# Token-per-row tokenizer and norms, and routing spread over the attention's batches

## The chip, the cores and the metric

The kernel runs on one core of a Trainium2 chip. Its time is the device time in microseconds (us) of the program, the median of three executions; the profile is of one further execution. The engines are TensorE (PE), VectorE (DVE), ScalarE (ACT), GpSimd (POOL) and SyncE (SP), each with its own instruction stream; they wait for each other on semaphores.

## The reference

An audio tower of two layers on x of 8 x 750 x 128, which the tokenizer turns into 8 batches (B) of 376 tokens of 256 numbers. What this change touches is the first layer up to the routing of the experts:

```python
y  = einsum('bpd,de->bpe', patches_16x16(x), tok_W) + tok_b
h  = (y - mean(y)) * rsqrt(var(y) + 1e-6) * gamma + beta          # tokenizer with its norm
n  = layernorm(h)                                                  # eps 1e-5
q, k, v = rope(n @ Wq), rope(n @ Wk), n @ Wv                       # 16 heads of 64
h  = h + softmax(causal(q k^T / 8)) v @ Wo + bo
xf = layernorm(h);  probs = softmax(xf @ router_w + router_b)      # 4 experts
top_p, top_i = top_k(probs, 2);  gates = top_p / sum(top_p)
h  = h + sum_e gates[e] * ((silu(xf @ w1[e]) * (xf @ w3[e])) @ w2[e])
```

Behind it comes a second layer, a complex linear recurrence over the tokens (`recurrence`) and a feed-forward block with quantised weights and activations (`quantised_ffn`); neither is changed, but for where the recurrence's tables are computed.

## The kernel before

Activations lie in SBUF with the 256 features over partitions in two halves and the tokens in columns; a batch is 376 columns. `audio_tower` calls the stages one after the other, each a block of the five engines' programs that ends in a barrier:

- `tokenize` (L187): matmuls (L220) of patches and weights, while VectorE makes the recurrence's tables of powers (`recurrence_tables`, L94).
- `layernorm` (L236) twice, for the tokenizer (ln_tok) and ahead of the attention (ln_attn). A token is a column, so sums over its features are matmuls against ones (L275, L285); the centring (L301) and the reciprocal of the deviation (L310), over 128x376, are VectorE's, the multiplication (L323) GpSimd's, squares, roots and the affine part ScalarE's (L336, L347, L341). With the second pass `split_weights` (L365) splits four weight matrices into a high and a low part on ScalarE (L372), VectorE (L379) and GpSimd (L387): all products of the kernel are made of such parts, as high x high + low x high + high x low.
- `attention` (L391): per batch eight steps `step(b, c)`, one for each pair of heads, and a `begin`. In a step TensorE projects Q or K of a later head (`project`, L496), computes scores (L508 mask, L518), turns the probabilities (`turn`, L533) and multiplies them by V (`mix`, L550); at a batch's end comes the output product (`output`, L572), 24 matmuls of 376 columns for each half of the features. ScalarE copies the projection (`raw`, L633), splits Q and K (`qk_high`, L639), makes the exponentials (`probs`, L646) and the high part of the turned probabilities (`pt_high`, L655). VectorE swaps pairs for the rotation (`swap_pairs`, L755/756), finds the maxima (L763), makes `pt_low` (L779) and adds the residual (L790). GpSimd rotates (L727, L729, L731) and makes `qk_low` (L716). Every engine's order is that of the code. A loop on the chip runs over the batches; the last is written out. SyncE first loads the tables, then clears the 12,288 rows of `x_slots` (L472, four transfers), then loads `resid` (L475) for each batch.
- `dispatch` (L872): all batches once more: each is turned to a token per row (L947, L1000), its norm is made with `bn_stats` (L1043, L1044) and a root on ScalarE (L1005), it is turned back (L956) for the router's product (L966), the two best experts and their gates are found, positions come from a prefix sum (L979), and GpSimd scatters the rows to `x_slots` (L1158, indirect transfers).
- `expert_tiles` (L1165), `recurrence` (L1488), `quantised_ffn` (L1810).

## Time and profile before

| | |
|---|---|
| three runs | 1922.29, 1924.59, 1925.28 us; median 1924.59 |
| the profiled execution | 1914.82 us, of which its span is 1913.0 |
| busy, share of the span | TensorE 83%, VectorE 64%, GpSimd 55%, ScalarE 53% |
| mean granted TensorE clock | 0.906 of 2.4 GHz |

The granted clock is what the chip let TensorE run at, as a share of its full speed; 0.5 of it is the lower of its two levels, 1.2 GHz. In a row of the lines' view stand the line, engine, operation, destination<-source and count, then the busy time, the mean duration in ns, and the idle time of the engine just before, with what ended it. The page's 40 slices, of 47.8 us each, show the stages:

```profile
## 2 busy tenths in 40 slices
PE   7749898989898989897728999999999926698329
...
DVE  6756565656565656564643666666655549658896
...
PEclk9869998999998999999558999999999957799659
DMA  5153000000000000000336555555555521103123
```

The first two or three digits are the front, then attention up to the 19th, then the routing at low clock, the experts, the recurrence and the feed-forward block.

### The profile page before, as it was taken

The numbers are of one execution on the slowest core, as the hardware profiler recorded it, in microseconds if no ns is written. First come the engines' busy times: TensorE is split into PE (matmuls) and PEld (weight loads), VectorE is DVE, ScalarE is ACT, GpSimd is POOL, SyncE is SP. The second block draws the span as 40 slices with busy tenths as digits, with TensorE's granted clock in tenths as the row PEclk, the third lists the DMA queues.
The fourth block names the chain that finished last, engine by engine and source line by source line (L and its number), as shares of the span: only waits on it lengthen the run. The fifth ranks groups of instructions, "written<-read, shape, count | busy, mean of one in ns | idle before, by whom it ended". The sixth has DMA issues, their size and how long they took to land. (4 is left out here: it accounts for less than half of the span.)

```text
span 1913.0 us, 32335 instructions
## 1 busy us (share of the span) xinstructions
PE 1589.7 (83%) x11205; PEld 1476.6 (77%) x11205; DVE 1221.8 (64%) x2397; ACT 1011.1 (53%) x2168; POOL 1055.0 (55%) x827
## 2 busy tenths in 40 slices
PE   7749898989898989897728999999999926698329
PEld 4338898989898989897628999999999915598219
DVE  6756565656565656564643666666655549658896
ACT  3536564656564656563615555555555524448562
POOL 0486767676767676762355776676777736300000
PEclk9869998999998999999558999999999957799659
DMA  5153000000000000000336555555555521103123
GB/s 192 65 176 118 1 8 0 8 0 8 0 8 0 8 0 8 0 9 4 107 109 214 142 138 147 139 138 143 143 145 144 149 75 33 33 1 118 66 75 114
DMA packets 74599, 142.85 MB, mean 75 GB/s; under 512 B 7400, under 2 KB 50728, under 8 KB 73992
## 3 DMA queue, kind: packets, MB, share of 16 engines
q1 hardware_dynamic: 63992, 127.80, 21.5%
q0 software_dynamic: 10512, 13.83, 4.2%
q8 instruction: 53, 0.87, 0.2%
q14 instruction: 42, 0.34, 0.1%
HBM read 108.15 MB, written 46.83 MB: 81 GB/s over the span
## 5 line engine op out<-in xcount | busy, mean ns | idle before, releaser
L1463 POOL TENSOR_TENSOR expert_w_low<-expert_raw,expert_w_high 128x768 fp32r<-128x768 f32 x152 | 289.5, 1958 | 157.6 <-ACT expert_w_high L1322 156.7
L646 ACT ACTIVATE probs<-psum,neg_max 120x376 f32<-120x376 f32 (+2 forms) x384 | 176.4, 479 | 140.1 <-DVE neg_max L763 140.1
L716 POOL TENSOR_TENSOR qk_low<-rotated,qk_high 128x376 fp32r<-128x376 f32 x128 | 138.3, 1081 | 180.2 <-ACT qk_high L639 175.9
L533 PE MATMUL psum<-diag,probs 128*128 128x128 f32 (+2 forms) x1536 | 203.5, 283 | 26.9 <-DVE pt_low L779 22.7
L533 PEld LDWEIGHTS psum<-diag,probs 128*128 128x128 f32 (+2 forms) x1536 | 185.5, 194 | 36.2 <-issue 25.5
L779 DVE TENSOR_TENSOR pt_low<-psum,pt_high 128x752 fp32r<-128x752 f32 x128 | 120.5, 941 | 142.5 <-ACT pt_high L655 141.5
L1439 DVE TENSOR_TENSOR expert_act_low<-expert_act,expert_act_high 128x384 fp32r<-128x384 f32 x152 | 148.6, 977 | 79.6 <-ACT expert_act_high L1360 79.6
L1360 ACT ACTIVATE expert_act_high<-expert_act 128x384 fp32r<-128x384 f32 x152 | 79.8, 525 | 171.4 <-DVE expert_act L1434 171.4
L1281 PE MATMUL psum<-slots_high,expert_w_high 128*128 128x384 f32 x608 | 157.9, 340 | 9.0 <-DVE expert_act L1434 7.8
L1281 PE MATMUL psum<-slots_low,expert_w_high 128*128 128x384 f32 x608 | 155.3, 336 | 0.0
L1281 PE MATMUL psum<-slots_high,expert_w_low 128*128 128x384 f32 x608 | 155.1, 336 | 0.0
L655 ACT ACTIVATE pt_high<-psum 128x752 fp32r<-128x752 f32 x128 | 102.6, 801 | 97.8 <-PE psum L533 95.9
L727 POOL TENSOR_TENSOR rotated<-raw,rope_cos 128x376 f32<-128x376 f32 x128 | 127.4, 995 | 39.4 <-ACT raw L633 25.5
L1322 ACT ACTIVATE expert_w_high<-expert_raw 128x768 fp32r<-128x768 f32 x152 | 126.6, 833 | 33.6 <-DMA expert_raw<-in_experts 33.6
L731 POOL TENSOR_TENSOR rotated<-rotated,swapped 128x376 f32<-128x376 f32 x128 | 138.6, 1083 | 10.0
L1292 PE MATMUL psum<-expert_w_high,expert_act_high 128*128 128x256 f32 x456 | 134.2, 294 | 5.3 <-ACT slot_out L1342 3.8
L1434 DVE TENSOR_TENSOR expert_act<-psum,silu 128x384 f32<-128x384 f32 x152 | 84.7, 557 | 77.3 <-ACT silu L1356 76.8
L729 POOL TENSOR_TENSOR swapped<-swapped,rope_sin 128x376 f32<-128x376 f32 x128 | 132.6, 1036 | 0.0
L1292 PE MATMUL psum<-expert_w_high,expert_act_low 128*128 128x256 f32 x456 | 128.5, 282 | 0.0
L1292 PE MATMUL psum<-expert_w_low,expert_act_high 128*128 128x256 f32 x456 | 128.4, 282 | 0.0
L763 DVE TENSOR_REDUCE neg_max<-psum 120x2 f32<-120x752 f32 (+2 forms) x192 | 119.4, 676 | 6.5 <-PE psum L518 6.5
L550 PE MATMUL psum<-pt_high,v_high 128*128 128x376 f32 (+2 forms) x384 | 113.8, 296 | 2.2 <-DVE pt_low L779 2.2
(303 smaller groups left out, 4549.4 us busy)
## 6 DMA issues: line engine op xcount, KB each, us to landing
expert_raw<-in_experts SPq DMA_DIRECT2D x152, 384.0 KB, 3.1
x_slots<-in_c_slots SPq DMA_DIRECT2D x4, 3168.0 KB, 27.9
slot_rows<-x_slots SPq DMA_DIRECT2D x19, 396.0 KB, 4.8
up_spill<-held SPq DMA_DIRECT2D x5, 1128.0 KB, 4.9
held<-up_spill SPq DMA_DIRECT2D x5, 1128.0 KB, 5.7
patch<-in_patches SPq DMA_DIRECT2D x4, 752.0 KB, 6.8
hid_spill<-hid SPq DMA_DIRECT2D x1, 3008.0 KB, 8.5
resid<-hid_spill SPq DMA_DIRECT2D x8, 376.0 KB, 3.5
```

The source lines that it names most:

```text
L533: last = pe.matmul(psum[0:nj, BANK_PT + bank, at:at + ni], probs[0:ni, h % 2, src:src + nj], diag[0:ni, h % 2, it, 0:ni], start=True, stop ...
L646: last = act.activation(probs[0:ni, h % 2, at:at + P * it + ni], score_bank(h % 2, it), ACT.Exp, bias=neg_max[0:ni, h % 2, it:it + 1], acc ...
L716: pool.tensor_tensor(qk[1][:, c % 2, k, :], rotated[:, k, :], qk[0][:, c % 2, k, :].bitcast(F32), ALU.subtract).then_inc(qk_ready, 1)
L727: pool.tensor_tensor(rotated[:, k, :], raw[:, k, :], cos[:], ALU.mult).then_inc(rope_made, 1)
L729: pool.tensor_tensor(swapped[:, k, :], swapped[:, k, :], sin[:], ALU.mult).then_inc(rope_made, 1)
L731: pool.tensor_tensor(rotated[:, k, :], rotated[:, k, :], swapped[:, k, :], ALU.add).then_inc(rot_made, 1)
L779: dve.tensor_tensor(pt[1][:, h % 2, :, :], psum[:, BANK_PT:BANK_PT + 2, 0:TOK], pt[0][:, h % 2, :, :].bitcast(F32), ALU.subtract).then_inc ...
L1281: last = pe.matmul(psum[:, 2 * k + g % 2, 0:TILE_SLOTS], w[hw][:, f, at:at + P], xt[hx][:, i % 2, c, :], start=(n == c == 0), stop=(n == 2 ...
L1292: last = pe.matmul(psum[:, BANK_DOWN + s, 0:DIM], act_hl[ha][:, g % 2, P * s:P * (s + 1)], w[hw][:, f, 4 * P:4 * P + DIM], start=(n == f = ...
L1322: act.activation(w[0][:, g % RING, :], raw[:, g % RAW, :], ACT.Copy).then_inc(w_high, 1)
L1439: dve.tensor_tensor(act_hl[1][:, g % 2, :], act_f[:, g % 2, :], act_hl[0][:, g % 2, :].bitcast(F32), ALU.subtract).then_inc(low_made, 1)
L1463: pool.tensor_tensor(w[1][:, g % RING, :], raw[:, g % RAW, :], w[0][:, g % RING, :].bitcast(F32), ALU.subtract).then_inc(w_low, 1)
```

## The change

`tokens_in` takes the place of `tokenize` and both passes of `layernorm`. A token is a row there, so mean and variance of both norms come from `bn_stats` on VectorE, the reciprocal is over 128x3, and ScalarE scales a row with its own factor and shift. The batches go through as a pipeline, `for i in range(BATCH + 3)`, in which the second norm of batch i-2 and the turning back of batch i-3 stand beside the first of batch i; the weights are split from i = 2 on. h and the norm's result are stored in DRAM and loaded by batch in the attention.

In `attention` all batches are written out (no loop on the chip). The output is made with tokens in rows, 3 tiles of 24 matmuls of 256 columns. `dispatch` is gone: the routing of batch b-1 stands in steps of batch b. Step 0 has its statistics, step 1 the root on ScalarE (which loads a table, and reloads the exponential's behind it), step 2 the scaling, 3 and 4 the turning, then the router's product, the odds' exponential, the choice, and in step 7 the positions; the scatter of batch b-2 stands in GpSimd's row in batch b, ahead of head 6. The last batch's routing follows at the stage's end. Seven small transfers with the router's parameters (`params`) are issued by SyncE between the clears of `x_slots` and the first `resid`; VectorE waits for all of them before its first batch. The recurrence's tables are begun in `tokens_in` and doubled in VectorE's row in the expert stage (chunks from 120 on).

The diff, cut (`route` calls the turning, the product and the prefix sum of TensorE by step; `seventh_read` only waits):

```diff
@@ tokens_in, SyncE (in place of tokenize and two layernorm passes) @@
+                for i in range(BATCH + 3):
+                    if here(i):
+                        sp.wait_ge(h_made, i + 1)
+                        many, few = token_rows(h0_rows, i)
+                        sp.dma_start(many, h[:, i % 3, 0:2, :]).then_inc(stored[i % 3], 16)
+                        sp.dma_start(few, h[0:TILE_ROWS[2], i % 3, 2, :]).then_inc(stored[i % 3], 16)
+                    if here(i - 3):
+                        sp.wait_ge(x_kept, i - 2)
+                        sp.dma_start(x_dram[:, :, tokens_of(i - 3)], xt[:, (i - 3) % 2, :, :]).then_inc(x_stored[(i - 3) % 2], 16)
...
@@ tokens_in, ScalarE @@
+                for i in range(BATCH + 3):
+                    if here(i):
+                        deviation(0, i)
+                    if here(i - 2):
+                        deviation(1, i - 2)
+                    if here(i):
+                        scale_tokens(i)
+                    if here(i - 2):
+                        scale_rows(i - 2)
+                    if here(i - 3):
+                        keep(i - 3)
+                    if 0 <= i - SPLIT_FROM < len(matrices):
+                        split_high(i - SPLIT_FROM)
...
@@ tokens_in, VectorE @@
+                for i in range(BATCH + 3):
+                    if here(i):
+                        biased(i)
+                        stat(0, i, y[:, i % 2, :, :])
+                    if here(i - 2):
+                        dve.wait_ge(h_made, i - 1)
+                        stat(1, i - 2, h[:, (i - 2) % 3, :, :])
+                    if here(i):
+                        inverse(0, i, h_scaled)
+                    if here(i - 2):
+                        inverse(1, i - 2, x_made)
+                    if 0 <= i - SPLIT_FROM - 1 < len(matrices):
...
@@ attention, SyncE @@
+                for b in range(2):
...
                     sp.dma_start(x_slots[e * CAPACITY:(e + 1) * CAPACITY, :], a["c_slots"]).then_inc(slots_cleared, 16)
-                with sp.Fori(0, BATCH) as b:
-                    sp.wait_ge(out_kept, 2 * b + CR_OUT)
...
+                sp.dma_start(bo[:], a["token_rows"][:, 3, :]).then_inc(params, 16)
...
+                sp.dma_start(before_f[:], a["c_before"]).then_inc(params, 16)
+                sp.dma_start(h_rows[TOKENS:TOKENS + TILE_SLOTS, :], a["c_slots"][0:TILE_SLOTS, 0:DIM]).then_inc(params, 16)
+                for b in range(BATCH + 1):
+                    if b:
+                        sp.wait_ge(out_kept, T * b)
+                    if b + 2 < BATCH:
+                        sp.wait_ge(attn_x_low, b + 1)
+                        sp.dma_start(xin[:, b % 2, :, :], x_dram[:, :, tokens_of(b + 2)]).then_inc(x_loaded[b % 2], 16)
+                    if b < BATCH:
+                        many, few = token_rows(h0_rows, b)
+                        sp.dma_start(resid[:, 0:2, :], many).then_inc(resid_in, 16)
+                        sp.dma_start(resid[0:TILE_ROWS[2], 2, :], few).then_inc(resid_in, 16)
+                    if b:
+                        many, few = token_rows(h_rows, b - 1)
+                        sp.dma_start(many, h[:, 0:2, :]).then_inc(h_stored, 16)
+                        sp.dma_start(few, h[0:TILE_ROWS[2], 2, :]).then_inc(h_stored, 16)
                 sp.wait_ge(slots_cleared, 16 * EXPERTS)
+                sp.wait_ge(params, 16 * 7)
+                sp.wait_ge(h_stored, 32 * BATCH)
 
...
@@ attention, TensorE, project(b, n) @@
-                        pe.wait_ge(out_kept, 2 * b + CR_OUT)
-                    w = (wq, wk)[k]
+                    if n == 2 * LEAD and b:
+                        pe.wait_ge(out_kept, T * (b - 1) + 2)
+                    if 2 * LEAD <= n and b:
+                        seventh_read(pe, b, (n - 1) // 2 - LEAD)
+                    wqk = (wq, wk)[k]
                     for i, (hw, hx) in enumerate(three):
...
+                def ahead_of(b):
+
+                    pe.wait_ge(chosen_made, b + 1)
+                    for k in range(T + 1):
+                        some = range(min(k + 1, T))
+                        for j in some:
+                            n = TILE_ROWS[j]
+                            m = TILE_ROWS[k] if k < T else P
+                            last = pe.matmul(prefix(b)[0:m, k, :], (before if j == k else ones_b)[0:n, 0:m],
...
@@ attention, TensorE, step(b, c, more) @@
                         values((0, 1))
+                    if b:
+                        if more or ahead < 2 * PAIRS:
+                            pe.wait_ge(raw_made, 16 * b + ahead + 1 + CR_RAW)
+                        else:
+                            pe.wait_ge(raw_made, 16 * (b + 1) + CR_RAW)
+                        route(b - 1, c)
                     turn(b, 2 * c + 1)
                     mix(b, 2 * c)
                     if more or ahead < 2 * PAIRS:
...
@@ attention, ScalarE @@
+                def deviation(b):
+                    act.wait_ge(summed, T * (b + 1))
+                    act.activation(std[:], moments[:, :, 1], ACT.Sqrt,
+                                   bias=consts[:, EPS_LN:EPS_LN + 1]).then_inc(std_made, 1)
+
+                def scale_rows(b):
+                    act.wait_ge(rstd_made, b + 1)
+                    if b:
+                        act.wait_ge(scattered, 32 * T * b)
+                    for k in range(T):
+                        n = TILE_ROWS[k]
+                        act.activation(rows[0:n, k, 0:DIM], h[0:n, k, :], ACT.Identity,
+                                       scale=rstd[0:n, k:k + 1], bias=shift[0:n, k:k + 1]).then_inc(x_made, 1)
+
...
+                    if b and c == 1:
+                        deviation(b - 1)
+                    if b and c == 2:
+                        scale_rows(b - 1)
+                    if b and c == ROUTE_LOGITS:
+                        odds_exp(b - 1)
...
@@ attention, GpSimd @@
+                def scatter(b):
+                    u = b % 2
+                    if b == 0:
+                        pool.wait_ge(slots_cleared, 16 * EXPERTS)
+                    pool.wait_ge(slots_made, b + 1)
+                    pool.wait_ge(gates_made, b + 1)
+                    pool.wait_ge(x_made, T * (b + 1))
+                    for k in range(T):
+                        n = TILE_ROWS[k]
+                        for j in range(2):
+                            pool.indirect_dma_start(
+                                x_slots, bass.IndirectOffsetOnAxis(ap=slots_u[0:n, u, j, k:k + 1], axis=0),
+                                rows[0:n, k, :], None).then_inc(scattered, 16)
+
...
+                for b in range(BATCH):
                     for n in range(2 * PAIRS):
+                        if n == 2 * LEAD and b >= 2:
+                            scatter(b - 2)
                         k = n % 2
...
@@ attention, VectorE, end of step(b, c, more) @@
+                    if b and c == 0:
+                        stat(b - 1)
+                    if b and c == ROUTE_LOGITS + 1:
+                        choose(b - 1)
+                    if c == ROUTE_LOGITS - 1:
+                        add_bo(b)
...
@@ attention, VectorE, before its first batch @@
+                x_split(0)
+                dve.memset(ones_b[:], 1.0).then_inc(routing, 1)
+                link(dve.memset(rows[:], 0.0))
+                dve.wait_ge(params, 16 * 7)
+                dve.tensor_copy(before[:], before_f[:]).then_inc(routing, 1)
                 dve.tensor_copy(base[:], const("region"))
...
-                        place_rows((i - 9) // T)
+                dve.wait_ge(tables_in, 64)
+                dve.tensor_copy(mask[:], mask_f[:]).then_inc(masks_made, 1)
+                dve.tensor_copy(ident_b[:], ident_f[:]).then_inc(masks_made, 1)
+                for n in range(2 * LEAD):
...
@@ expert_tiles, VectorE, after the work of chunk g @@
+                    at = g - FIRST_TABLE
+                    if at == 0:
+                        follow(dve.tensor_copy(turn[:, :, :, 0], first[:]))
+                    if 0 <= at < 2 * DOUBLINGS:
+                        double_turns(at // 2, at % 2)
+                    if 2 * DOUBLINGS <= at < 2 * DOUBLINGS + HALVES:
+                        feeds(at - 2 * DOUBLINGS)
...
```

What stands in VectorE's row where attention begins; before, `x_low` is the first batch's split, `mask` and `ident_b` are made of the loaded tables, and L756 is `swap_pairs`:

```order
L750 TENSOR_TENSOR x_low<-held,x_high 128x752 [waits x_high,cleared]
L827 CAST mask<-mask_f 128x256 [waits tables_in]
L828 CAST ident_b<-ident_f 128x256
L755 MEMSET holder 128x1 [waits raw_made]
L756 STREAM_SHUFFLE swapped<-raw 128x376
```

And now:

```order
L956 TENSOR_TENSOR x_low<-attn_x_in,x_high 128x752 [waits attn_x_high,cleared]
L1156 MEMSET ones_b 128x128
L1157 MEMSET x_rows 128x792
L1159 CAST before<-before_f 128x128 [waits route_params,route_step_made]
L1160 COPY slot_base<-moe_consts 128x4
L1162 CAST mask<-mask_f 128x256 [waits tables_in]
L1163 CAST ident_b<-ident_f 128x256
L961 MEMSET holder 128x1 [waits raw_made]
L962 STREAM_SHUFFLE swapped<-raw 128x376
```

Four instructions were put ahead of the masks, and the first of the casts waits for `params`; the swaps stand behind it.

ScalarE's row at the end of step 1 and the beginning of step 2 of a batch before, and now:

```order
L633 ACTIVATE raw<-psum 128x376 [waits rot_made,proj_made]
L637 REGISTER_ALU
L639 ACTIVATE qk_high<-rotated 128x376 [waits scores_made,rot_made]
L660 ACTIVATE o_high<-psum 128x376 [waits mixed]
L655 ACTIVATE pt_high<-psum 128x752 [waits mixed,turned]
L633 ACTIVATE raw<-psum 128x376 [waits rot_made,proj_made]
L646 ACTIVATE probs,row_sum<-psum,neg_max 120x376 [waits max_made,turned]
```

```order
L786 ACTIVATE raw<-psum 128x376 [waits rot_made,proj_made]
L792 ACTIVATE qk_high<-rotated 128x376 [waits scores_made,rot_made]
L813 ACTIVATE o_high<-psum 128x376 [waits mixed]
L817 ACT_TABLE_LOAD
L817 ACTIVATE row_std<-row_moments,consts 128x3 [waits route_summed]
L808 ACTIVATE pt_high<-psum 128x752 [waits mixed,turned]
L786 ACTIVATE raw<-psum 128x376 [waits rot_made,proj_made]
L799 ACT_TABLE_LOAD [waits max_made]
L799 ACTIVATE probs,row_sum<-psum,neg_max 120x376 [waits turned]
```

Two table loads and the root stand between `o_high` and the next `probs`.

GpSimd's row between the heads 5 and 6 of a batch, before and now (from the third batch on):

```order
L731 TENSOR_TENSOR rotated<-rotated,swapped 128x376 [waits rope_made]
L716 TENSOR_TENSOR qk_low<-rotated,qk_high 128x376 [waits qk_high]
L725 REGISTER_ALU
L727 TENSOR_TENSOR rotated<-raw,rope_cos 128x376 [waits qk_ready,raw_made]
L729 TENSOR_TENSOR swapped<-swapped,rope_sin 128x376 [waits swap_made]
```

```order
L934 TENSOR_TENSOR rotated<-rotated,swapped 128x376 [waits rope_made]
L903 TENSOR_TENSOR qk_low<-rotated,qk_high 128x376 [waits qk_high]
L916 DMA x_slots<-x_rows,slots_u 12288x264 [waits route_gates_made,route_x_made,route_slots_made,slots_cleared]
L916 DMA x_slots<-x_rows,slots_u 12288x264 x5
L930 TENSOR_TENSOR rotated<-raw,rope_cos 128x376 [waits qk_ready,raw_made]
L932 TENSOR_TENSOR swapped<-swapped,rope_sin 128x376 [waits swap_made]
```

Six scatters stand between one head's `qk_low` and the next head's rotation.

## Rows read from the trace of the kernel before

**Rows 1.** Windows by stage: length, busy us, granted clock, DMA share, GB/s.

```profile
0.00:117.00 117.00, 70.69 (x192) 39.39 (x192) 85.86 (x145) 49.52 (x72) 39.46 (x24) 0.85 0.27 105
117.00:147.00 30.00, 22.30 (x72) 17.78 (x72) 9.02 (x29) 8.70 (x16) 23.90 (x24) 0.63 1.00 320
147.00:904.50 757.50, 712.90 (x5977) 673.14 (x5976) 471.16 (x1073) 438.75 (x1257) 507.18 (x491) 0.98 0.03 10
904.50:1001.50 97.00, 46.90 (x264) 39.73 (x264) 53.74 (x277) 40.97 (x94) 46.99 (x48) 0.51 0.32 104
```

**Rows 2.** Timeline, SyncE's queue, attention begins: start, duration, queue, line.

```profile
118.77 2.65 SPq L472 DMA_DIRECT2D x_slots<-in_c_slots  x4
121.79 0.64 SPq L475 DMA_DIRECT2D resid<-hid_spill  x1
```

**Rows 3.** Tile `resid`: its transfers from issue to landing.

```profile
DMA to landing us min/median/max: 3.4/3.5/41.6
```

**Rows 4.** Timeline where attention begins, VectorE and TensorE.

```profile
124.63 0.57 DVE L756 STREAM_SHUFFLE swapped<-raw 128x376 f32<-128x376 f32 x1
...
147.01 0.51 PE L508 MATMUL psum<-mask,ident_b 64*128 64x128 bf16 x12
```

**Rows 5.** Lines, 0 to 117 us: busy us, mean ns | idle before.

```profile
L310 DVE RECIPROCAL ln_attn_rstd<-ln_attn_std 128x376 f32<-128x376 f32 x8 | 19.7, 2480 | 0.9 <-ACT ln_attn_std L347 0.9
...
L301 DVE TENSOR_TENSOR hid<-hid,psum 128x752 f32<-128x752 f32 (+1 forms) x8 | 7.2, 900 | 10.3 <-PE psum L275 10.3
...
L379 DVE TENSOR_TENSOR L_attn_Wv_low<-L_attn_Wv_staged,L_attn_Wv_high 128x1536 fp32r<-128x1536 f32 x1 | 2.8, 2810 | 0.0
```

**Rows 6.** Lines, 904.5 to 1001.5 us, the stage `dispatch`.

```profile
L1158 POOL DMA_INDIRECT x_slots<-x_rows,slots_u x48 | 47.0, 979 | 69.2 <-DVE slots_u L1097 56.4 <-issue 12.5 <-DVE x_rows L1084 0.3
...
L966 PE MATMUL psum<-router_w,router_x 128*128 128x4 f32 (+1 forms) x96 | 20.4, 318 | 0.5 <-ACT router_x L1013 0.5
L956 PE MATMUL psum<-ident,x_rows 128*128 128x128 f32 (+1 forms) x48 | 16.0, 437 | 17.5 <-DVE x_rows L1050 17.5
...
L1043 DVE BATCH_NORM_STATS2 row_stats<-h_tm 128x6 f32<-128x256 f32 (+1 forms) x24 | 10.1, 421 | 6.4 <-ACT h_tm L1000 6.4
...
L1005 ACT ACT_TABLE_LOAD x7 | 9.0, 1283 | 0.1
...
L979 PE MATMUL psum<-chosen,ones_b 128*128 128x4 bf16 (+2 forms) x48 | 4.6, 190 | 0.0
L1044 DVE BATCH_NORM_AGGREGATE row_moments<-row_stats 128x2 f32<-128x6 f32 (+1 forms) x24 | 4.4, 182 | 0.8
...
L979 PE MATMUL psum<-chosen,before 128*128 128x4 bf16 (+1 forms) x24 | 3.8, 197 | 3.0 <-DVE chosen L1079 2.9
```

**Rows 7.** Timeline of one attention step: GpSimd, VectorE, TensorE.

```profile
731.05 1.00 POOL L727 TENSOR_TENSOR rotated<-raw,rope_cos 128x376 f32<-128x376 f32 x1 [2.06 <-ACT raw L633]
...
736.86 1.53 PE L533 MATMUL psum<-diag,probs 128*128 128x128 f32 x12
...
737.22 1.16 POOL L716 TENSOR_TENSOR qk_low<-rotated,qk_high 128x376 fp32r<-128x376 f32 x1 [3.17 <-ACT qk_high L639]
...
739.26 0.94 DVE L779 TENSOR_TENSOR pt_low<-psum,pt_high 128x752 fp32r<-128x752 f32 x1 [0.39 <-ACT pt_high L655]
...
741.04 1.16 PE L533 MATMUL psum<-diag,probs 128*128 128x128 f32 x8
```

**Rows 8.** Timelines of TensorE and ScalarE, up to the batch's end.

```profile
745.84 1.53 PE L533 MATMUL psum<-diag,probs 128*128 128x128 f32 x12
...
790.00 0.52 ACT L639 ACTIVATE qk_high<-rotated 128x376 fp32r<-128x376 f32 x1 [3.88 <-POOL rotated L731]
...
792.70 0.57 PE L533 MATMUL psum<-diag,probs 128*128 128x128 f32 x3 [2.89 <-DVE pt_low L779]
```

**Rows 9.** Tile `slots_u`: indirect scatters from issue to landing.

```profile
DMA to landing us min/median/max: 2.4/2.6/3.8
```

**Rows 10.** Line 1471: duration ns min/median/max of GpSimd's indirect transfers.

```profile
L1471 POOL DMA_INDIRECT h_rows<-slot_out,slot_ids x57: 1550/1690/1710, 1051.5 to 1542.0; - x57
```

1129 lines of the change are left out of this document (528 added, 601 removed).

## Prediction

> **What bounds the kernel now.** I read four views, coarse to fine. First the windows by stage [rows 1]. From 0 to 117 us (tokenizer, two norms, splitting the weights) VectorE is the busiest engine, 85.86 of 117 us. From 147 to 904.5 us, the body of the attention, TensorE is busy 712.90 of 757.50 us at a granted clock of 0.98, that is at the 2.4 GHz level: this stage is TensorE's, and GpSimd (507) and VectorE (471) stand behind it. From 904.5 to 1001.5 us, the routing stage, no engine is busy for even 60% of the time and TensorE's clock is 0.51, the 1.2 GHz level: this is a stage of handoffs. So the first and the fourth stretch can be cut, and what is put into the third is paid for unless it fits between TensorE's instructions.
>
> Second, the lines of the first stretch [rows 5]: the reciprocal over 128x376 costs 2.48 us and runs 16 times, 39.5 us of VectorE, to give one number per token. Third, the timeline of an attention step [rows 7, 8]. `turn` of even heads starts at 736.86 and at 745.84: 8.98 us a step. In it GpSimd waits 2.06 us before L727 and 3.17 us before L716, both for ScalarE, so GpSimd has no long reserve of its own; between two heads it is only a fraction of a microsecond ahead of the chain that feeds ScalarE's `qk_split`. `pt_low` ends at 739.26 + 0.94 = 740.20, the `turn` that follows starts at 741.04: 0.84 us of slack. Where the batch ends that slack is gone: TensorE stands 2.89 us for `pt_low` at 792.70, behind ScalarE, which stood 3.88 us for GpSimd's `rotated` at 790.00. Fourth, the start of the attention [rows 2 to 4], where the DMA engines are busy throughout (share 1.00 in [rows 1]).
>
> **The change part by part.** The sum is made against the profiled execution, 1914.8 us; the median of the runs is 1924.6, 0.5% above it.
>
> *Front.* With a token per row a norm's statistics are 3 `bn_stats` and 3 aggregates per batch, and the reciprocal is over 128x3. VectorE has per batch one addition over 752 columns (0.90, L301 in [rows 5]), two sets of statistics of 3 x 0.42 + 3 x 0.18 = 1.8, a little overlapped 1.7 [rows 6], and two small reciprocals with their shift, about 0.4 each: 5.1, and I take 5.3 for contention. Batches 0 and 1 have no second norm beside them, 3.6 each; six are at 5.3, 31.8; the first sums come at about 10.5; four weight splits in VectorE's row cost 1.7 to 3.3, around 2.3 each (2.81 for one in [rows 5]), 9.2; behind the last batch its second norm goes through VectorE, ScalarE, TensorE, a store and the stage's barrier, about 16. That is 10.5 + 7.2 + 31.8 + 9.2 + 16 = 74.7 in place of 117: -42.5. Bounds: -50 if the splits hide, -30 if ScalarE's and TensorE's chain per batch does not keep up.
>
> *A wait before the first batch.* Seven small transfers (`params`) are issued by SyncE behind the four clears of `x_slots`, and VectorE now waits for all seven before it casts the mask and makes the first `swap_pairs`; behind that wait stand all its rotations, hence GpSimd, ScalarE and the first scores. The row beside it: `resid`, issued at 121.79 behind the same clears, landed 41.6 us later [rows 2, 3], at 163.4, while every other one of the eight took 3.4 or so. `resid` wasn't needed then; `params` are. Counted from the stage's beginning at 117.0 [rows 1], the first `swap_pairs` ran 7.6 us in, at 124.63 [rows 4], and `resid` came 46.4 us in; I take 51 to 52 for the last of `params`, since seven transfers are issued and one of them writes 384 rows in DRAM. That is 51.6 - 7.6 = +44. The first scores, at 147.01 [rows 4], move by the same. Bounds: 0, if the small ones land in their 3.4 us, and +50. I take +44, because the one transfer behind those clears that the trace shows did wait for them.
>
> *TensorE's added work in the body.* Per batch: 12 logit matmuls of 0.318 twice over 8 batches is 20.4 / 8 = 2.55, the turning 16.0 / 8 = 2.0, the prefix (4.6 + 3.8) / 8 = 1.05 [rows 6], all at clock 0.51; 5.6 at half clock is 2.8 at 0.98. The output now comes as 24 x 3 matmuls of 256 columns, 18,432, for 18,048: 0.15 us. With the switch of operands between them I take 3.1, seven times: +22. TensorE is the bound there, so all of it counts. Bounds: +14 if the small ones overlap, +39 at half clock.
>
> *Waits added in the body.* Three inserts per batch, in three engines' rows, seven batches each:
> - ScalarE: a table load before the root (1.283 [rows 6]), the root, and a load again before the next exponential, together about 3.0 us ahead of `pt_high` and `probs`. The step has 0.84 us of slack at `pt_low` [rows 7] and some idle time of ScalarE before it: I take 2.0 of 3.0, 14 in all.
> - GpSimd: six indirect scatters of 0.979 [rows 6], with their issue (47.0 + 12.5) / 48 = 1.24 each, 7.5 us in one piece, ahead of `rotated` of head 6. Its idle time within the step is 2.06 + 3.17 = 5.2 [rows 7], so 2.3 us are late, six times (the last two batches' scatters stand elsewhere): 14. Beside VectorE's work an indirect transfer of the same form takes 1.69 instead of 0.98 [rows 10]; then the piece is nearer 12 and the delay 6.6.
> - ScalarE's `scale_rows` (3 activations, about 1.1) 0.6 x 7 = 4; VectorE's small chunks (statistics 1.7, choice 1.25, place 1.1) in its idle time, 0.4 x 7 = 3; register instructions of the old loop gone, -1.
> Sum +34. Bounds: 0, if TensorE's own added work of 3.1 us is where the others catch up, and +83 (below).
>
> *The tail in place of the routing stage.* 97.0 us [rows 1] go. In their place one batch goes through alone: statistics 1.7, root 0.3, inverse 0.4, scaling 1.1, turning 2.0, its copy 0.5, logits 2.7, weighing 0.65, table and exponential 1.5, choice 1.25, prefix 0.65, place 1.1, six scatters 7.5, landing 2.6 [rows 9], the gap that lies today between the last landing and the next stage 5.0, handoffs 1.5: 30.5. (Prefix, weighing, choice and placing are three to seven instructions of 0.16 to 0.21 us each, as the small ones in the view of [rows 6].) That is 97.0 - 30.5 = 66.5, call it -67. Bounds: -72 and -58 (scatters at 1.69 [rows 10] and half-clock handoffs).
>
> *Recurrence tables* move from the front, where they lay beside the tokenizer's DMAs, into VectorE's idle time in the expert stage: +1, between 0 and +5.
>
> Sum: -42.5 + 44 + 22 + 34 - 67 + 1 = -8.5, 1906.3 for a profiled execution, and with the 0.5% of the median above it **1916**.
>
> **The rivals.**
> *The wait at the start doesn't happen.* All the small transfers land in about 3.5 us like the seven later `resid` [rows 3] and only the queue's 7 issues are added. For: they are a few hundred descriptors against the clears' 12,288 rows. Against: the first `resid` is small too, and waited 41.6. The 44 us fall away: 1872.
>
> *The body absorbs its inserts.* TensorE's 3.1 us stand in the same steps as the inserts on ScalarE and GpSimd, and GpSimd's lateness is made up in its idle 5.2 us of each step after it. Against it speaks the stand of 2.89 us at 792.70, which GpSimd causes today without any insert. The 34 us fall away: 1882.
>
> *Slower: the inserts are paid in full.* GpSimd is needed once per head, and ScalarE, which feeds it, waits for it in turn; if the two are so locked that neither regains what it lost, each insert is a delay for TensorE: 5.4 on ScalarE (3.0, 1.1 for `scale_rows`, 1.3 for the load at the odds' exponential) and 3.1 on TensorE, seven times, and 7.5 on GpSimd, six times: 59.5 + 45 = +105 in place of +56. That is 49 more: 1965. The place is head 6 of each batch from the third on, where the scatters stand ahead of `rotated`. It decides from the point at which GpSimd's delay exceeds the chain's slack of 0.84 us and the idle time of the same step isn't usable, since it lies after ScalarE's own wait.
>
> *A longer table switch.* The trace has 14 table loads in the routing stage, 1.283 us each, with idle 0.1 before them [rows 6], and I count them so. If each switch cost 1.38 us more, 14 switches on ScalarE's path in the body would add 19: 1935. The Trainium skill, page "ScalarE: Activation LUTs", section "What ACT_TABLE_LOAD costs", says just that: about 1283 ns for the load and about 1380 ns for a drain. This trace agrees with the first number and shows no row for the second.
>
> **How the numbers follow.** Forecast 0.45, inserts in full 0.25, body absorbs 0.15, no wait at the start 0.10, longer switch 0.05. The forecast's own range, from its uncertain terms (front -30 to -50, waits in the body by some 15 either way), is 1898 to 1936. The range to 8 in 10 takes in the absorbing body below and, above, most of the way to the slower rival: 1882 to 1955. What a measurement can tell from no change is 0.2%, 3.9 us. Faster by more is below 1920.7: 0.25 of the forecast's 0.45, and the two cases below with 0.25, 0.50. Within 0.2% (1920.7 to 1928.5): 0.12 of the forecast's. Slower: its last 0.08, the inserts and the switch, 0.38.
>
> **What would show each step.** The attention's first DMA at about 75 us instead of 117. VectorE's first `swap_pairs` 45 to 55 us behind it, released by the transfers and not by ScalarE; if it follows in under 12 us, the second term is wrong. The windows of the body: its batch period 95 now, about 103 forecast (22 + 34 over seven), 98 if absorbed, 110 if in full; TensorE's idle time there put down to `pt_low` and `qk_low`, in the step of the scatters. From the last residual to the first transfer of the expert stage 30 us. The forecast is wrong if the body's period lies outside 99 to 107 or the start's wait outside 38 to 50.

## The result and the profile after

The changed kernel took 1938.71 us (median of four runs, 1933.20 to 1942.99) against 1924.09 for the kernel before; the ratio is 1.0072, interval 1.0047 to 1.0097. I forecast 1916 with a range of 1882 to 1955: the time lies inside the range, but the sign was wrong. Run again on another chip, the ratio was 1.0046 (1.0029 to 1.0062). The kernel before took 1925.3 us on the chip of e1 to e4 and 1913.1 and 1913.6 on those of the later timed runs, so runs are compared by their ratios and, within a trace, by stages.

The windows by stage of the changed kernel (stretch, length, busy us of the engines, granted clock, DMA share, GB/s), cut at the attention's beginning, its first `swap_pairs`, its last residual, the expert stage's first transfer and the recurrence's first load:

```profile
0.00:76.00 76.00, 36.88 (x144) 29.44 (x144) 50.12 (x178) 44.47 (x80) 35.55 (x27) 0.77 0.53 189
76.00:125.30 49.30, 6.71 (x18) 5.26 (x18) 3.21 (x11) 1.80 (x3) 3.68 (x3) 0.50 0.95 320
125.30:973.00 847.70, 770.29 (x6411) 717.41 (x6411) 568.88 (x1323) 478.37 (x1334) 562.94 (x553) 0.95 0.05 17
973.00:1000.50 27.50, 4.78 (x27) 4.25 (x27) 7.76 (x44) 4.34 (x8) 5.90 (x6) 0.57 0.13 44
1000.50:1569.80 569.30, 518.72 (x3342) 500.77 (x3342) 361.53 (x602) 283.71 (x526) 374.27 (x209) 0.97 0.52 137
```

They answer to [rows 1]. The expert stage, which [rows 1] don't show, was this in the kernel before, in the same view:

```profile
1001.50:1551.00 549.50, 512.92 (x3342) 496.93 (x3342) 324.18 (x521) 284.74 (x526) 374.08 (x209) 0.98 0.55 145
```

For the same 3342 matmuls the stage takes 19.8 us longer, and VectorE has 81 instructions and 37 us of busy time more.

| stretch | before | after | difference | forecast |
|---|---|---|---|---|
| start to the attention's beginning | 117.0 | 76.0 | -41.0 | -42.5 |
| on to the first `swap_pairs` | 7.6 | 49.3 | +41.7 | +44 |
| on to the last residual | 779.8 | 847.7 | +67.9 | +56 |
| on to the expert stage's first transfer | 97.1 | 27.5 | -69.6 | -67 |
| expert stage | 549.4 | 569.2 | +19.8 | +1 |
| the rest | 362.0 | 361.6 | -0.4 | 0 |
| sum | 1913.0 | 1931.4 | +18.4 | -8.5 |

The start, in the timelines of SyncE's queue and of VectorE (start, duration, line; in brackets the idle time before and what ended it):

```profile
79.42 3.28 SPq L534 DMA_DIRECT2D x_slots<-in_c_slots  x4
82.74 0.83 SPq L535 DMA_DIRECT2D attn_bo<-in_token_rows  x1
...
86.22 24.86 SPq L541 DMA_DIRECT2D h_rows<-in_c_slots  x1
```

```profile
124.71 0.23 DVE L1159 CAST before<-before_f 128x128 bf16<-128x128 f32 x1 [42.14 <-DMA h_rows<-in_c_slots]
...
125.34 0.57 DVE L962 STREAM_SHUFFLE swapped<-raw 128x376 f32<-128x376 f32 x1
```

VectorE stands 42.14 us for the last of the seven small transfers, and the first swap comes at 125.34, 0.7 us later than in [rows 4], though the stage begins 41 us earlier: what the front gained was given back whole.

In the body, `turn` starts give the length of each half step. The third batch with routing, beside the one of the kernel before (us from one `turn` to the next, two for a step):

| step | 0 | | 1 | | 2 | | 3 | | 4 | | 5 | | 6 | | 7 and the next `begin` | |
|---|---|---|---|---|---|---|---|---|---|---|---|---|---|---|---|---|
| before | 4.1 | 4.8 | 4.2 | 4.8 | 4.2 | 4.8 | 4.2 | 4.8 | 4.2 | 4.8 | 7.8 | 5.0 | 7.1 | 4.9 | 8.0 | 17.6 |
| after | 4.1 | 7.1 | 4.6 | 5.0 | 4.8 | 6.2 | 4.7 | 5.3 | 4.6 | 4.8 | 7.7 | 4.8 | 7.3 | 6.4 | 8.3 | 18.0 |

TensorE's timeline at steps 0 and 2 of that batch:

```profile
462.77 1.58 PE L627 MATMUL psum<-diag,probs 128*128 128x128 f32 x12
468.66 0.44 PE L644 MATMUL psum<-pt_high,v_high 128*128 128x376 f32 x1 [2.07 <-DVE pt_low L985]
469.91 1.54 PE L627 MATMUL psum<-diag,probs 128*128 128x128 f32 x12
...
484.32 1.55 PE L627 MATMUL psum<-diag,probs 128*128 128x128 f32 x12 [0.49 <-DVE pt_low L985]
489.26 0.44 PE L644 MATMUL psum<-pt_high,v_high 128*128 128x376 f32 x1 [1.15 <-DVE pt_low L985]
490.50 1.54 PE L627 MATMUL psum<-diag,probs 128*128 128x128 f32 x12
```

Step 0's second half is 7.14 instead of 4.80 us and holds the six scatters; step 2's is 6.18 and holds a table load. Steps 3 and 4 grow by TensorE's own additions. In step 5 the two rows don't compare: the 7.8 us of the kernel before fell into a stretch at the lower clock, and its batches without one took 6.4 there, while the 7.7 after is at full clock (more on this under r8). TensorE's additions are, in the instructions by line from 255 to 880 us, six batches:

```profile
L686 PE MATMUL psum<-router_w,router_x 128*128 128x4 f32 (+1 forms) x72 | 10.1, 269 | 0.0
L676 PE MATMUL psum<-ident,x_rows 128*128 128x128 f32 (+1 forms) x36 | 6.5, 290 | 0.0
L698 PE MATMUL psum<-chosen,ones_b 128*128 128x4 bf16 (+2 forms) x36 | 2.6, 174 | 0.0
L698 PE MATMUL psum<-chosen,before 128*128 128x4 bf16 (+1 forms) x18 | 2.4, 179 | 0.0
```

That is 21.6 / 6 = 3.6 us a batch.

What grew in the expert stage, in VectorE's and GpSimd's timelines of one chunk (L1456 and L1460 are a step of the recurrence's tables, two instructions each):

```profile
1482.75 0.56 DVE L1486 TENSOR_TENSOR expert_act_low<-expert_act,expert_act_high 128x384 fp32r<-128x384 f32 x1 [0.59 <-ACT expert_act_high L1377]
1483.22 0.41 DVE L1456 TENSOR_SCALAR turn_tmp<-recur_turn 128x64 f32<-128x64 f32 x2
1483.67 1.97 DVE L1460 SCALAR_TENSOR_TENSOR recur_turn<-recur_turn,turn_tmp 128x64 f32<-128x64 f32 x2
1485.68 0.56 DVE L1481 TENSOR_TENSOR expert_act<-psum,silu 128x384 f32<-128x384 f32 x1
```

```profile
1483.53 1.84 POOL L1514 TENSOR_TENSOR expert_w_low<-expert_raw,expert_w_high 128x768 fp32r<-128x768 f32 x1 [2.17 <-ACT expert_w_high L1339]
```

Two instructions over 64 columns take 1.97 us and end 0.27 us after GpSimd's split of a weight chunk does. `expert_act`, on which TensorE waits, starts the moment they are done, with no idle time before it. In the kernel before that instruction mostly had 0.33 to 1.43 us of idle time ahead of it, here 0.82:

```profile
1465.65 0.56 DVE L1434 TENSOR_TENSOR expert_act<-psum,silu 128x384 f32<-128x384 f32 x1 [0.82 <-ACT silu L1356]
```

### The profile page after: what moved, and what is told of

Its sections match the earlier page's. It is cut to its first block and busy times, and to the rows that moved or that the text cites. A ratio compares the mean times of both kernels' runs of the same rounds, so it can differ in the third digit from the quotient of the medians.

```text
span 1931.4 us, 31390 instructions
## 1 busy us (share of the span) xinstructions
PE 1560.6 (81%) x11301; PEld 1466.0 (76%) x11301; DVE 1269.3 (66%) x2510; ACT 1001.1 (52%) x2154; POOL 1045.7 (54%) x830
## 5 line engine op out<-in xcount | busy, mean ns | idle before, releaser
L627 PE MATMUL psum<-diag,probs 128*128 128x128 f32 (+2 forms) x1536 | 211.0, 290 | 31.7 <-DVE pt_low L985 27.3
L627 PEld LDWEIGHTS psum<-diag,probs 128*128 128x128 f32 (+2 forms) x1536 | 191.9, 201 | 39.3 <-ACT raw L786 22.6
L1486 DVE TENSOR_TENSOR expert_act_low<-expert_act,expert_act_high 128x384 fp32r<-128x384 f32 x152 | 140.2, 923 | 79.6 <-ACT expert_act_high L1377 79.0
L644 PE MATMUL psum<-pt_high,v_high 128*128 128x376 f32 (+2 forms) x384 | 118.3, 308 | 22.9 <-DVE pt_low L985 22.9
L934 POOL TENSOR_TENSOR rotated<-rotated,swapped 128x376 f32<-128x376 f32 x128 | 131.1, 1024 | 10.0
```

Of the source, the lines that this page charges most:

```text
L627: last = pe.matmul(psum[0:nj, BANK_PT + bank, at:at + ni], probs[0:ni, h % 2, src:src + nj], diag[0:ni, h % 2, it, 0:ni], start=True, stop ...
L934: pool.tensor_tensor(rotated[:, k, :], rotated[:, k, :], swapped[:, k, :], ALU.add).then_inc(rot_made, 1)
L1486: dve.tensor_tensor(act_hl[1][:, g % 2, :], act_f[:, g % 2, :], act_hl[0][:, g % 2, :].bitcast(F32), ALU.subtract).then_inc(low_made, 1)
```

## The experiments

My theory after the two traces: three things cost independently of each other, the wait for `params`, the scatters' place, and the table steps, which are held by GpSimd. The rival for the first two was that removing a wait only uncovers the next; for the third, that VectorE's steps are too long by themselves.

**e1: the small transfers first.**

```diff
+                sp.dma_start(bo[:], a["token_rows"][:, 3, :]).then_inc(params, 16)
...
+                sp.dma_start(h_rows[TOKENS:TOKENS + TILE_SLOTS, :], a["c_slots"][0:TILE_SLOTS, 0:DIM]).then_inc(params, 16)
                 for e in range(EXPERTS):
                     sp.dma_start(x_slots[e * CAPACITY:(e + 1) * CAPACITY, :], a["c_slots"]).then_inc(slots_cleared, 16)
-                sp.dma_start(bo[:], a["token_rows"][:, 3, :]).then_inc(params, 16)
...
```

> The changed kernel with one edit: SyncE issues the seven small params transfers ahead of the four clears of x_slots instead of behind them. Theory (the clears hold the small transfers back, and VectorE's wait for them is the whole delay at the start): the first swap_pairs comes about 10 us after the stage's first DMA instead of 49.3, the stages behind move up together, and the time falls by 38 to 42 us, to about 1898 (ratio to before 0.987). Rival (the first batch would have been held by the clears anyway, through the tables' or x's transfers or DMA contention): under 15 us are gained.

1897.33 us, ratio 0.9852 (0.9828 to 0.9876). VectorE's wait, in its timeline, is now short:

```profile
85.44 0.23 DVE L1159 CAST before<-before_f 128x128 bf16<-128x128 f32 x1 [3.26 <-DMA h_rows<-in_c_slots]
...
86.07 0.57 DVE L962 STREAM_SHUFFLE swapped<-raw 128x376 f32<-128x376 f32 x1
```

The first swap comes at 86.07, 10.5 us after the stage's first DMA. The same seven transfers, the same bytes, 39 us earlier: that much of the wait was their place behind the clears. The 3.26 us that remain keep the first swap 2.9 us later in the stage than in the kernel before (7.6). This edit alone makes the changed kernel 1.5% faster than the one before.

**e2: the scatters one place earlier.**

```diff
-                        if n == 2 * LEAD and b >= 2:
-                            scatter(b - 2)
...
                                            ALU.add).then_inc(rot_made, 1)
+                        if n == 2 * LEAD - 1 and b >= 2:
+                            scatter(b - 2)
                         if n:
                             qk_split(b, n - 1)
```

> The changed kernel with one edit: the six scatters of batch b-2 stand in GpSimd's row before qk_low of head 4 (where GpSimd is idle 9.02 us at 763.88, waiting for ScalarE's qk_high) instead of after it, ahead of the rotation of head 6. Theory (GpSimd's 7.5 us in one piece delay the step behind them): the second half of step 0 goes from 7.1 back to 4.8 us, and step 1's from 5.7 to 4.7 where it was longer, in six batches: 14 to 20 us less, about 1922. Rival (the batches grew for ScalarE's and TensorE's inserts, and time given back in step 0 is lost in the waits of the following steps): under 5 us.

1920.39 us, ratio 0.9964 (0.9949 to 0.9980), that is 1.1% less than the changed kernel. GpSimd's timeline ahead of the sixth batch's `qk_low`, from the last of the six scatters:

```profile
660.54 0.99 POOL L916 DMA_INDIRECT x_slots<-x_rows,slots_u  x1 [0.30 <-issue]
666.68 1.16 POOL L903 TENSOR_TENSOR qk_low<-rotated,qk_high 128x376 fp32r<-128x376 f32 x1 [5.15 <-ACT qk_high L792]
```

The six scatters lie in GpSimd's idle time, of which 5.15 us are left. Step 0's second half is 4.8 in all batches; the stretch from the first to the last `turn` went from 804.1 to 790.1 us. The forecast's own term for the scatters had been 14, but this 14.0 is a balance. Steps 0 and 1 gave back 20.3 us in the six batches, some 6 of them (an estimate) because 13.7 us at the lower clock fell into these steps before and none now, and each of the six batches' ends became 1.2 us longer (the half step with the next `begin` takes 19.2 in place of 18.0), which it does not in r8 with the same edit. What was moved is a wait that the trace doesn't explain. In step 0 of the changed kernel TensorE's 2.07 us are spent on `pt_low`, which waited for ScalarE's `pt_high` and not for GpSimd's late rotation. ScalarE's line there, and the same one of r1 (the changed kernel on another chip, below):

```profile
466.83 0.80 ACT L808 ACTIVATE pt_high<-psum 128x752 fp32r<-128x752 f32 x1 [2.01 <-remote]
```

```profile
461.81 0.80 ACT L808 ACTIVATE pt_high<-psum 128x752 fp32r<-128x752 f32 x1 [0.37 <-PE psum L627]
```

`remote` is a release for which the trace has no instruction. In the changed kernel VectorE's second maximum and ScalarE's `pt_high` have such waits, of up to 2.7 and 2.0 us, in just the six batches with scatters in step 0, and in e2 VectorE's maximum has them at the ends of the six batches where the scatters now stand. In r1 the scatters end just as late (2.9 us after `turn` starts), there is no such wait, and the half step takes 5.3 to 5.5 us. So on that chip the scatters' lateness on GpSimd costs 0.5 to 0.7 us a batch, and the rest of the 2.3 goes with these waits, whose cause stays open.

**e3 and e4: the table steps cut and moved, and left out.** e3 makes each step two parts of two instructions, in two chunks from the 104th on, ahead of the wait for `high_made`; e4 deletes the steps.

```diff
                     if i and f == KEEP_AT:
                         keep_out(i - 1)
+                    elif g >= TABLES_FROM and tables[0] <= 4 * DOUBLINGS + 2 * HALVES:
+                        table_part(tables[0])
+                        tables[0] += 1
                     dve.wait_ge(high_made, g + 1)
...
-                    if 0 <= at < 2 * DOUBLINGS:
-                        double_turns(at // 2, at % 2)
```

> The changed kernel with one edit: the recurrence tables' steps in the expert chunks are cut in two parts, tensor_scalar and scalar_tensor_tensor, and each stands in VectorE's row between expert_act (L1481) and expert_act_low (L1486), where VectorE waits 0.59 us for ScalarE and GpSimd's weight split (L1514) has not begun, in 41 of the last 48 chunks, instead of behind expert_act_low in 20. Theory (GpSimd's split and VectorE's instructions with two operands in SBUF shut each other out, so a table instruction of 0.25 us takes up to 1.9): the table instructions fall to 0.2 to 0.4 us each and the stage from its first DMA to the recurrence's first load from 569 to 549-553 us: 16 to 20 us less, about 1921. Rival (the steps' own instructions and waits are too long for VectorE's row): they now stand directly on the path to expert_act_low, and the stage stays at 565 or more.

> The changed kernel without the table steps in the expert chunks (turn and feed are only set to zero once, ahead of the first tile: the recurrence's tables are left out). Theory (the 20 us by which the expert stage grew are all the table steps'): the stage falls from 569 to 549-551 us, the time to about 1920. Rival (part of the growth is from the clearing of semaphores moved into GpSimd's row or from GpSimd's added work): it stays above 556.

e3: 1917.49 us, ratio 0.9949 (0.9933 to 0.9966), expert stage 551.7 us. e4: 1915.19 us, ratio 0.9947 (0.9930 to 0.9963), expert stage 549.4, as before the change. So all of the 19.8 us were the table steps'. But e3 was right for a reason I had only half: I expected 0.2 to 0.4 us an instruction, and in the lines by form some still took several times that.

```profile
L1459 DVE SCALAR_TENSOR_TENSOR recur_turn<-recur_turn,turn_tmp 128x64 f32<-128x64 f32 x4 | 5.7, 1463 | 0.0
...
L1462 DVE TENSOR_SCALAR turn_tmp<-recur_turn 128x2 f32<-128x2 f32 x4 | 5.4, 1385 | 0.0
...
L1462 DVE TENSOR_SCALAR turn_tmp<-recur_turn 128x1 f32<-128x1 f32 x4 | 0.6, 202 | 0.0
```

Two columns cost 1385 ns on average where one costs 202, and 64 columns cost 1463: the amount of work doesn't decide. Nor is the one column merely lucky in its place. The changed kernel's trace has both kinds just behind the start of a split:

```profile
1434.49 1.84 POOL L1514 TENSOR_TENSOR expert_w_low<-expert_raw,expert_w_high 128x768 fp32r<-128x768 f32 x1 [0.42 <-ACT expert_w_high L1339]
...
1434.61 0.34 DVE L1456 TENSOR_SCALAR turn_tmp<-recur_turn 128x1 f32<-128x1 f32 x2
...
1434.98 1.50 DVE L1460 SCALAR_TENSOR_TENSOR recur_turn<-recur_turn,turn_tmp 128x1 f32<-128x1 f32 x2
...
1441.28 1.86 DVE L1456 TENSOR_SCALAR turn_tmp<-recur_turn 128x2 f32<-128x2 f32 x2
```

In the traces of the eleven runs that have table steps and the full split, 22 `tensor_scalar` of one column began inside a split and all 22 took about 0.2 us; all 72 of two or more columns, and all 157 `scalar_tensor_tensor` of any width, ran until the split had ended. Most parts of e3 are still held where they meet a split, but a held part fits in a chunk where a held whole step does not. The next two runs separate place, size and hold.

**e11 and e12: a shorter split on GpSimd; the parts in the old place.**

```diff
+                    cols = 2 * P if CHUNKS * (N - 4) <= g else 6 * P
-                    pool.tensor_tensor(w[1][:, g % RING, :], ...
+                    pool.tensor_tensor(w[1][:, g % RING, 0:cols], ...
```

> The changed kernel in which GpSimd's weight split (L1514) takes 256 in place of 768 columns in the last 32 chunks, those with the table steps (the low parts of the rest are left as they were: part of the computation is left out). Theory (a table instruction is held while GpSimd's split runs): the pairs of scalar_tensor_tensor in the table steps fall from 1.9 to under 1.1 us and the stage from 569 to 550-556 us. Rival (VectorE's steps are too long by themselves): the pairs stay at 1.9 and the stage at 565 or more.

> The changed kernel with the table steps cut in the 41 parts of e3, but each behind expert_act_low, where GpSimd's split has begun. Theory (each part that overlaps the split is held until its end, however short it is): the stage stays at 560 to 575 us, no better than the 20 whole steps. Rival (the sum of work per chunk decides, and half a step fits in the idle 1.8 us): 549 to 553, as e3.

Each of the two ran once. e11: the stage takes 548.8 us with all the table steps where they were. L1460 in the lines of 1430 to 1555 us, of the changed kernel and then of e11:

```profile
L1460 DVE SCALAR_TENSOR_TENSOR recur_turn<-recur_turn,turn_tmp 128x1 f32<-128x1 f32 (+8 forms) x36 | 30.2, 879 | 0.6
```

```profile
L1460 DVE SCALAR_TENSOR_TENSOR recur_turn<-recur_turn,turn_tmp 128x1 f32<-128x1 f32 (+8 forms) x36 | 14.2, 433 | 0.6
...
L1515 POOL TENSOR_TENSOR expert_w_low<-expert_raw,expert_w_high 128x256 fp32r<-128x256 f32 x29 | 21.8, 752 | 54.9 <-ACT expert_w_high L1339 47.2 <-DVE slot_ids L1415 7.7
```

Nothing on VectorE was changed, and its instructions halved, because GpSimd's took 0.75 us where in the timeline of the changed kernel above it took 1.84. The shorter split can't have sped the stage up by itself, since e4 reaches 549.4 with the full one. That settles the hold: these VectorE instructions, when they begin inside GpSimd's `tensor_tensor`, wait for its end (but for the one-column `tensor_scalar`). The Trainium skill, page "SBUF — State Buffer", section "Who interferes with whom", states it as an exclusive lock on a port pair that VectorE and GpSimd share, held for a whole instruction; the trace agrees. Not every VectorE instruction is held. The kernel before shows it for two that run once a chunk beside the same split, one with an input in PSUM, one with both in SBUF (duration min/median/max):

```profile
L1434 DVE TENSOR_TENSOR expert_act<-psum,silu x152: 545/558/561, 1017.4 to 1533.9; 128x384 f32<-128x384 f32 x152
...
L1439 DVE TENSOR_TENSOR expert_act_low<-expert_act,expert_act_high x152: 542/774/3570, 1018.6 to 1535.1; 128x384 fp32r<-128x384 f32 x152
```

Of the 84 `expert_act_low` that began inside a split all ran to its end, of the 108 `expert_act` none. So the hold could be read from the trace of before, in the very stage to which the tables were moved. e12: 555.1 us, between what I gave the theory (560 to 575) and the rival (549 to 553). Where a part stands matters for 3.4 us of the stage; that it is half a step, and spread over 41 chunks in place of 20, matters for 14. So it is the hold together with the size of the piece, and the expectation that one of them decides alone was wrong.

**e5: no table switch.**

```diff
-                    act.activation(std[:], moments[:, :, 1], ACT.Sqrt,
+                    act.activation(std[:], moments[:, :, 1], ACT.Identity,
```

> The changed kernel with the root in the attention's routing replaced by ScalarE's Identity (the reciprocal of the variance in place of that of the deviation: part of the computation is changed), so that ScalarE switches no table: 14 loads less in the stage. If a switch costs its row of 1.283 us, of which I counted 2.0 of 3.0 us a batch on the path, steps 1 and 2 give back 1 to 2 us in seven batches, 7 to 14 in all, about 1928. If each switch costs 1.38 us more (a drain), 20 to 30 us. If the loads lie beside waits, 0 to 3 us.

1908.11 us, ratio 0.9972 (0.9960 to 0.9985), beside 1.0046 for the changed kernel on a like chip (r1 below; e10, which changes nothing that can be told, has 1.0050 on e5's own): 0.7%, 14 us. From the first to the last `turn` it is 773.8 us against r1's 787.5, 13.7 less. Step 2 is back at 4.2 and 4.8. The forecast had 14 for this term. ScalarE's timeline at the loads in the changed kernel:

```profile
480.92 1.28 ACT L817 ACT_TABLE_LOAD   x1
482.21 0.30 ACT L817 ACTIVATE row_std<-row_moments,consts 128x3 f32<-128x3 f32 x1
...
485.58 1.28 ACT L799 ACT_TABLE_LOAD   x1 [2.00 <-DVE neg_max L969]
486.88 0.57 ACT L799 ACTIVATE probs<-psum,neg_max 120x376 f32<-120x376 f32 x1
```

The activation starts 0.01 us after its load ends. There is no further 1.38 us in or behind the load, and the rival that I built on them is out.

**e10 and e9: the bias addition moved,** alone and on top of e8.

```diff
-                    if c == ROUTE_LOGITS - 1:
+                    if c == PAIRS - 1:
                         add_bo(b)
```

> The changed kernel with only that addition moved to the end of step 7: 8 to 11 us less than the changed kernel, about 1929, or nothing by the rival.

> e8 with VectorE's addition of the output bias to the residual moved from the end of step 4 to the end of step 7. It takes 1.47 + 1.21 us there (L1004, L1006), twice what 512 and 256 columns need, ahead of pt_low of step 5, beside GpSimd's row. Theory: at the batch's end GpSimd is idle, the two additions take 0.7 + 0.4 us and nothing waits; step 5's first half goes from 9.2 to 7.7 us, 7 x 1.5 = 8 to 11 us less than e8, about 1848. Rival (TensorE's wait in step 5 is for x_low alone): no change.

e10: 1923.80 us, ratio 1.0050 (1.0034 to 1.0067), the same as the changed kernel's 1.0046. e9: 1858.30, ratio 0.9711 (0.9695 to 0.9727), e8's is 0.9724. No gain that can be told. In e9 the 128x512 addition fell from 1471 to 886 ns, the 120x256 one stayed at 1224, and step 5's first half still took 7.7 in some batches and 9.2 in others: TensorE's wait there (1.86 us for `x_low` in every batch) isn't the addition's doing. This theory fell, and what 9.2 and 7.7 differ by is shown under r8.

**e8 and r8, with r1: the three edits together,** and the changed kernel beside them.

> The edits of e1, e2 and e3 together. Theory (three places, one behind the other in time, that don't cover each other): the sum, -41 -18 -21 = -80, about 1858, ratio to before 0.965. Rival (what one gives back the next stage takes): 1875 or more.

> The changed kernel itself, beside e8's edits on the same chip, since the single edits were timed on one chip and their sum on another, where step 0 with its scatters took 5.5 us in place of 7.2. It should again be 0.5 to 0.8% above the kernel before; on a chip with the short step 0 about 0.2%.

> The three edits of e8 again, beside the changed kernel on the same chip. If the three gains add up there (theory), it is 4.0 to 4.6% below the changed kernel where step 0 takes 7.2 us, and 3.5 to 4.0% where it takes 5.5, since the scatter's place is then worth less. If the gains cover each other, under 3.3%.

e8: 1860.37 us, ratio 0.9724 (0.9708 to 0.9741). The 1858 that I expected was nearly met only because the kernel before takes 12 us less on that chip; by the ratio, 0.965, I missed it by 0.7%. r1: 1922.25 us, ratio 1.0046, where I expected 0.2% above for a chip with the short step 0. r8: 1861.36 us, ratio 0.9726 (0.9705 to 0.9747), so 0.9726 / 1.0046 = 0.968 of the changed kernel. That is 61 us less where the singles on the other chip summed to 87 (1.0072 less 0.9852, 0.9964 and 0.9949: 4.5%). Two of r8's windows, cut as above, of the body and the expert stage:

```profile
86.30:918.70 832.40, 771.18 (x6419) 718.62 (x6417) 569.13 (x1324) 477.49 (x1335) 562.00 (x553) 0.95 0.10 32
...
946.20:1498.40 552.20, 514.05 (x3342) 497.99 (x3342) 365.85 (x602) 284.62 (x526) 377.74 (x209) 0.98 0.53 141
```

Beside r1's trace (first swap at 124.55, expert stage 568.9) two of the gains are there whole: -38.2 and -16.7. The third isn't: from first to last `turn` r8 takes 786.8 us and r1 787.5. On r1's chip step 0's second half took 5.3 to 5.5 us and not 7.1, so the scatters' place was worth at most 6 x 0.6 = 4 us, and this much came back in step 5, whose first half was 9.2 or more in five of six batches of r8 and 7.7 in four of six of r1. I expected 3.5 to 4.0% below the changed kernel and it was 3.2%, which I had written down for the case that the gains cover each other; by the stages they don't, but one of them is smaller there. Step 5 doesn't wait for anything different in these batches. Two windows of r8 over its first half, of the second and the third batch with routing:

```profile
365.93:375.11 9.18, 7.32 (x63) 6.57 (x61) 8.75 (x16) 3.85 (x9) 6.33 (x5) 0.81 0.00 0
469.45:477.15 7.70, 5.83 (x62) 5.27 (x61) 7.32 (x14) 3.19 (x7) 6.34 (x5) 1.00 0.01 2
```

TensorE's wait for `x_low` is 1.86 us in both. The granted clock is 0.81 in the one, 1.00 in the other: the trace's clock records have 3.4 us at the lower level in it. So it is in all 24 of these half steps in the changed kernel, r1, r8 and e9: 7.7 us where the clock is 1.00, 9.2 where it is 0.81, 9.9 to 10.3 at 0.73 to 0.76. From the first to the last `turn` the kernel before has 34 us at the lower level, the changed kernel 65, r1 49 and r8 60. At 1.5 us for 3.4, the 11 us by which r8 exceeds r1 are worth about 5, an estimate from these half steps, and that is what the moved scatters seemed to lose. Why the stretches at the lower level fall where they do, no run shows.

Step 0 differs between the chips by the waits shown under e2: the runs beside a kernel before of about 1924 or 1925 us have them, those beside 1913 us don't.

e8, e9 and r8, at 1858 to 1861 against 1913 for the kernel before, are the fastest found, 2.7 to 2.9% below it.

## Why the prediction was wrong

- **The step that failed** is the last term of the sum, "Recurrence tables ... into VectorE's idle time in the expert stage: +1, between 0 and +5". It was 19.8. I had the step's length from instructions that ran while GpSimd was idle, and VectorE's idle time from the chunk, and didn't look at what GpSimd does in that idle time. It runs its weight split there, and a step beside it is held to about 2.4 us. I took [rows 10] (GpSimd's transfers at 1.69 us where they took 0.98 in [rows 6]) for a disturbance by VectorE and used it only for the scatters; at `expert_act_low`, 0.54 to 3.57 us in that stage of the kernel before, I didn't look. e4 shows the whole of it is the steps', e11 that the hold is the cause. Put 19.8 in place of 1, and the sum is -8.5 + 18.8 = +10.3, or 1935 for the median: slower, as it came. My list of signs had none for the expert stage, and none of those it had went off: the batches took 102.3 to 107.2 us, 105 on average, and the start's wait was 42.
- **The body** was 11.9 us under-sized, and its parts don't hold as I summed them. The table loads were right: 14 (e5: 13.7). TensorE's added work was too low: 3.6 us a batch for routing, where half of the durations at half clock had given 2.8. A logit matmul takes 0.252 us in the stretches at the upper level and 0.351 in those at the lower one, 0.269 on average; it took 0.318 in the routing stage of before, and the half of that was wrong. The output took 58.5 us in six batches for 55.6 before, 0.5 a batch for the 0.15 that I had. Together 4.1 x 7 = 29 for 22. For the clock I had no term: the body had 80 us at the lower level for 52 before, and the 28 more are worth some 12 us, an estimate at 1.5 us for 3.4.
- **The scatters** were right by luck. I had 14, for GpSimd 2.3 us late six times, and step 0 did grow by 2.3, but r1 shows that this lateness is worth 0.5 to 0.7 of it; the rest, on one kind of chip only, goes with waits of an unknown cause. With the scatters at their 14, the 7 more for TensorE and some 12 for the clock make 19 and not 11.9, so something else of the +34 was too high, `scale_rows` and VectorE's small chunks (7 together) for one; no run prices them. The additions of the bias, not priced at all, cost nothing that can be told (e10).
- **The wait at the start** was right in mechanism and size, 44 against 41.7, and e1 shows it. It alone did not decide the sign: e1, e2, e3 and e4, each one edit, are all faster than the kernel before.
- **The front** (-42.5 against -41.0) and **the tail** (-67 against -69.6) were right within their bounds, the front 76.0 us for the 74.7 of the sum, the tail 27.5 for 30.5.
- **The rivals**: the inserts were not paid in full (the body at +68, not +105), nor absorbed, the wait happened, the longer switch did not. My range held the time; the 0.38 for slower was too little, since the term that failed had no rival and bounds of 0 to +5.

## What to carry to other kernels

Before work is moved into an engine's idle time, look at what its neighbours do in just that time. A VectorE instruction with two inputs in SBUF, or a `tensor_scalar` of two or more columns from SBUF, that began inside GpSimd's `tensor_tensor` was held to its end here, so price it by what is left of GpSimd's instruction, and cut the work into pieces that fit even when held. One instruction's min and max far apart in the trace of before are the sign. Issue what a stage's first instruction waits for ahead of bulk clears on the same queue. When an insert is put in an engine's row, look for the place one or two instructions away where that engine is already waiting. And before a difference between two traces is put down to a wait, compare the granted clock of just that stretch.

## What the hardware showed beyond that

- A switch of ScalarE's table costs its 1.283 us load and nothing visible behind it (next activation after 0.01 us); seven batches with two switches each cost 13.7 us of time, 2.0 a batch.
- The logit matmuls, with 4 output columns, follow the clock less than in proportion: 0.252 us in the stretches at the upper level, 0.351 in those at the lower, in the same trace.
- A `tensor_scalar` of one column runs in 0.2 us inside GpSimd's split; one of two columns was held to its end (1.86 us for two of them).
- SyncE itself stood 24.86 us issuing the transfer behind the clears (86.22), so a queue full of clears delays not only landings but the issues behind it; in e1 that issue took 0.60 us.
